# 3x3 convolutions contracted over 128 rows, with partition copies by GpSimd's DMAs

## The chip, the cores and the metric

The kernel runs on one core of a Trainium2 chip. The metric is device time in microseconds (us). The kernel before takes 3841.41 us, the median of three runs (3840.19 to 3842.67). Engines are PE (TensorE, matmuls), DVE (VectorE), ACT (ScalarE), POOL (GpSimd) and SP (SyncE, which issues most DMAs). In the trace PEld is PE's weight loading.

## The reference

The input x has 8 images of 96 channels of 96 x 96 pixels in float32. Two blocks, each with a residual sum, follow one another:

```
x = x + L0(gn(x))       # gn: group norm over 32 groups of 3 channels
x = x + L1(gn(x))

L0: four depthwise 7-tap filters (row, column, two diagonals) -> feats[4]
    context = mean(feats^2); hid = leaky_relu(context @ att1); a = softmax(hid @ att2 over the 4)
    out = conv3x3(sum_d a[d] * feats[d], w_proj)            # 96 -> 96 channels

L1: q, k, v = 1x1 convs; softmax over pixels of q and k; a linear attention; 1x1 conv; 1x1 conv to k, v;
    depthwise 3x3 conv; a second attention whose query goes through an FFT; 1x1 conv
```

In the kernel all linear maps of L1 that follow softmax(q) are folded into one 3x3 convolution per image with 96 x 96 x 9 weights `a32`, applied to E = exp(q). So each image passes through two 3x3 convolutions over 96 channels: the first with the fixed weights `wp` (L0), the second with `a32` (L1).

## The kernel before

Images go through a software pipeline. `steps` calls `start(0)`, `step(0)`, a loop of `step(b)` for b = 1 to 6, `step(7)` and `step(8)`. Every `step(b)` does the second block of image b-1 (`second`) and the first block of image b (`first`) on all five engines; each engine has its own program and keeps its own order, and semaphores order them against each other.

PE's program for one step is: the maxima of k and q (`maxes`), the rows of the FFT, k and v, the context (about 200 us together), the q tiles, then the second convolution of image b-1, then the first convolution of image b, then the group sums. DVE runs beside it: the depthwise taps of image b (L715, in 12 `unit`s of 12 taps of 96x1536), with short pieces for PE between, then `attention_weights` (L750), the last three units of taps with the split of E between them, then `attention` (L806), the products of the four directions with their weights (`products`, L823), and the sums that make x1 (`x1_sum`, L795). During the last of these it starts on image b+1.

A 3x3 convolution (`conv`, L954) goes over 12 blocks `j` of 8 image rows, each in two halves of 4 rows (384 columns). Values are split in a high and a low part in the reduced type that PE reads in one pass: image e_hi + e_lo, weights hi + lo. A half is 27 matmuls over 96 rows: nine taps times (hi x e_hi, hi x e_lo, lo x e_hi). Blocks alternate between two PSUM slots. In the second convolution block j needs the copy of block j-2 out of PSUM, by ACT (`final_copy`, waited for at L1083); in the first convolution it needs the x1 sum of block j-2, by DVE (L1141).

ACT's program between these (L630 to L646) runs in this order: final_copy 0 and 1, `unit_work(b, 9)`, copies 2 and 3, `unit_work(b, 10)`, copies 4 and 5, `unit_work(b, 11)`, copies 6 to HID_AT (7), the softmax of the direction attention, then the high parts of the first convolution's input (`fg_high`), chunk by chunk of 16 rows, with the last copies between. `unit_work(b, u)` squares the unit's two directions and so waits for DVE's taps of unit u.

The direction attention of image b is served by PE inside the second convolution of image b-1: `hidden` (eight tiny matmuls) before half (7, 1), `logits` before half (8, 0). `hidden` waits for DVE's sums over the squares (L811); DVE then waits for `hidden` (L813) and `logits` (L817) before the first product (L832).

DVE's x1 sums stand at fixed places: after chunks 3, 4 and 5 of the products, then between the statistics and the first taps of image b+1. After the twelfth sum the group norm follows, ACT normalizes x1, and the next step begins with `maxes`. POOL issues the loads of `res`, the stores of x1 and the accumulating stores of the result, in program order.

Of the kernel before, what the change touches and what calls it, by code (L numbers as in the profile page):

```python
# [84 lines left out]
HID_AT = 7  # L85
# [4 lines left out]
L0_SMALL, L1_SMALL, GN_SMALL = 8, 21, 7  # L90
# [36 lines left out]
def build(nc, a, out):  # L127
    with ExitStack() as ctx:
# [3 lines left out]
        def sem(name):  # L132
# [8 lines left out]
        e_hi = nc.alloc_sbuf_tensor_at("e_hi", [C, EN], F32R, offset=lo0)  # L141
        e_lo = nc.alloc_sbuf_tensor_at("e_lo", [C, EN], F32R, offset=lo0 + EBYTES)
# [16 lines left out]
        vrow = sb("vrow", [W, VROWS, TR, C])  # L159
        etile = sb("etile", [C, ETILES, TR * W])  # L160
        krow = etile[0:W, 0:VROWS].rearrange("p s (r c) -> p s r c", c=C)
        wp_hi, wp_lo = sb("wp_hi", [C, 9, C], F32R), sb("wp_lo", [C, 9, C], F32R)
        a_hi = sb("a_hi", [C, 9, C], F32R)
# [3 lines left out]
        a_lo = nc.alloc_sbuf_tensor_at("a_lo", [C, 9, C], F32R, offset=k0)  # L167
        bk = nc.alloc_sbuf_tensor_at("bk", [C, 9, C], F32, offset=k0 + ABYTES)

        squares = [nc.alloc_sbuf_tensor_at(f"squares{n}", [C, CR * W], mybir.dt.bfloat16, offset=k0 + n * ABYTES)  # L170
                   for n in range(2)]
        assert CR * W * 2 <= ABYTES
# [70 lines left out]
        fin_ready, fin_copied = sem("fin_ready"), sem("fin_copied")  # L243
        waits_passed = {e.engine: sem(n) for e, n in (
# [13 lines left out]
        def rows(buf, r0, n, dx=0):  # L258

            at = (r0 + 1) * EP + 1 + dx  # L260
            return buf[:, at:at + n * EP].rearrange("p (r c) -> p r c", c=EP)[:, :, 0:W]
# [126 lines left out]
        def _(pool):  # L388
# [5 lines left out]
            def zero_pads():  # L394
                for e in (e_hi, e_lo):
                    f = e[:, :].bitcast(F32)
                    pool.memset(f[:, 0:EP], 0.0).then_inc(pads_zero, 1)
                    pool.memset(f[:, (H + 1) * EP:EN], 0.0).then_inc(pads_zero, 1)
                    pool.memset(f[:, EP:EP + H * EP].rearrange("p (r c) -> p r c", c=EP)[:, :, 0:1], 0.0)\
                        .then_inc(pads_zero, 1)  # L400

# [3 lines left out]
            def step(b, first, second, more):  # L405
                if second:
                    i = b - 1
                    pool.wait_ge(gram_done, i + 1)
                    apart(pool)
                    zero_pads()  # L410
                    pool.wait_ge(l1_small, i * L1_SMALL + 5)
                    pool.tensor_tensor(l1v[:, 1:2], l1v[:, 0:1], consts[:, 1:2], ALU.pow).then_inc(l1_pow, 1)
                    o = image(out, i)
                    for j in range(NG):
                        pool.wait_ge(fin_copied, i * NG + j + 1)
                        if j == 0:
                            apart(pool)
                            pool.wait_ge(x1_stored, (i + 1) * NG * 16)
                        apart(pool)
                        pool.dma_start(o[:, j * GR * W:(j + 1) * GR * W], res[:, j % RES], accum_op=ALU.add)\  # L420
                            .then_inc(out_stored[j % RES], 16)
                if first:
                    if not second:
                        zero_pads()
                    x, o = image(a["x"], b), image(out, b)
                    for j in range(NG + 1):
                        if j < NG:
                            if j < RES:
                                wait(pool, out_stored[j], b * (NG // RES) * 16)
                            else:  # L430
                                wait(pool, x1_done, b * NG + j - RES + 1)
                            apart(pool)
                            pool.dma_start(res[:, j % RES], x[:, j * GR * W:(j + 1) * GR * W])\
                                .then_inc(res_loaded[j % RES], 16)
                        if j >= 1:
                            pool.wait_ge(x1_done, b * NG + j)
                            apart(pool)
                            pool.dma_start(o[:, (j - 1) * GR * W:j * GR * W], x1[0:C, (j - 1) * GR * W:j * GR * W])\
                                .then_inc(x1_stored, 16)
                        if more and j == GN_AT:  # L440
                            start(b + 1)
                    gn_pow(gnx1_small, GN_SMALL, b, 5, 2, gnx1_pow)
# [14 lines left out]
        def _(act):  # L457
# [4 lines left out]
            act.activation(wp_hi[:], wp32[:], ACT.Identity).then_inc(wp_hi_ready, 1)  # L462
# [38 lines left out]
            def square(b, u, d):  # L501
# [7 lines left out]
                act.activation(squares[0 if first_image(b) else 1][:], feat[:, d], ACT.Square, accum_out=sq[:, d, ch:ch + 1]).then_inc(squared, 1)  # L509
# [145 lines left out]
        def _(dve):  # L655
            taps_w = [lambda k: wh[:, k:k + 1], lambda k: wv[:, k:k + 1],
                      lambda k: w45[:, k * KT + k:k * KT + k + 1],
                      lambda k: w135[:, k * KT + KT - 1 - k:k * KT + KT - k]]
            def set_up():
# [3 lines left out]
                dve.wait_ge(wp_hi_ready, 1)  # L663
                dve.tensor_tensor(wp_lo[:], a32[:], wp_hi[:].bitcast(F32), ALU.subtract).then_inc(wp_ready, 1)
# [85 lines left out]
            def attention_weights(i, chain):  # L750
# [41 lines left out]
                dve.wait_ge(a_hi_ready, i + 1)  # L792
                st(dve.tensor_tensor(a_lo[:], a32[:], a_hi[:].bitcast(F32), ALU.subtract))
# [129 lines left out]
        def _(pe):  # L923
# [30 lines left out]
            def conv(i, whi, wlo, done, ready, between={}, low_ready=lambda: None):  # L954

                for j in range(NG):
                    ready(j)
                    for h in range(2):
# [59 lines left out]
            def attention_block(i, between):  # L1018
# [65 lines left out]
                conv(i, a_hi, a_lo, fin_ready, ready, between, lambda: pe.wait_ge(l1_small, i * L1_SMALL + 21))  # L1084
# [23 lines left out]
            def step(b, first, second, more):  # L1108
# [17 lines left out]
                if second:  # L1126
                    attention_block(b - 1, {(HID_AT, 1): hidden, (HID_AT + 1, 0): logits} if first else {})
# [3 lines left out]
                if first:  # L1131
                    if not second:
                        pe.wait_ge(wp_ready, 1)

                    def ready(j):
                        pe.wait_ge(fg_ready, b * NCH + min(NCH - 1, (j + 1) * GR // CR) + 1)
# [5 lines left out]
                    conv(b, wp_hi, wp_lo, conv_ready, ready, {(GN_AT + 1, 0): lambda: start(b + 1)} if more else {})  # L1142
# [58 lines left out]
```

## Time and profile before

| | us |
|---|---|
| median of the runs | 3841.41 |
| the profiled execution | 3844.74 |
| its span, first to last instruction | 3843.1 |
| PE busy | 3649.9 (95%) |
| DVE busy | 3024.8 (79%) |
| ACT busy | 1642.1 (43%) |
| POOL busy | 211.1 (5%) |

Busy time counts every instruction from its start to its end; matmuls are pipelined, so two overlap in the rows and the step from one start to the next is what one costs. "L715" is a line of the kernel. A row of a timeline gives start, duration, engine, line, operation, output<-input, and in brackets how long the engine was idle before it and what ended that.

### The profile page before, as it was taken

What the parts mean: (1) busy time and instruction counts of PE and PEld (TensorE: products, weight loads), DVE (VectorE), ACT (ScalarE), POOL (GpSimd) and SP (SyncE); (2) the same over time, 40 slices, a digit from 0 to 9 for tenths busy, and PEclk for the clock granted to TensorE, in tenths of its full rate; (3) what the DMA queues carried; (4) which work ended last, traced back from release to release, by engine and by line L of the source; (5) the groups of instructions that cost most, each with busy time, mean ns of one, the idle gap of its engine ahead of it and who ended that gap; (6) DMA issues with size and microseconds to landing.
All of it is one profiled execution on the core that took longest, in us unless ns stands there. A gap on an engine that the chain in (4) does not pass through costs nothing.

```text
span 3843.1 us, 59619 instructions
## 1 busy us (share of the span) xinstructions
PE 3649.9 (95%) x22946; PEld 2998.9 (78%) x22946; DVE 3024.8 (79%) x2829; ACT 1642.1 (43%) x2720; POOL 211.1 (5%) x376
## 2 busy tenths in 40 slices
PE   4659999999999999999999999999999999999998
PEld 2348688968789688886889687896888878897977
DVE  7988998789877898779987898878987798854020
ACT  3422682138521584126821386215841268211630
POOL 1001000100001000010001000010000100010000
PEclk8779999999999999999999999999999999999999
DMA  5355222922147231742229222471317422271002
GB/s 116 98 137 132 66 67 35 225 73 69 48 102 182 59 83 42 167 121 67 66 37 226 71 68 51 110 182 48 87 41 173 112 67 66 39 178 32 1 7 31
DMA packets 164730, 344.35 MB, mean 90 GB/s; under 512 B 110336, under 2 KB 110576, under 8 KB 164432
## 3 DMA queue, kind: packets, MB, share of 16 engines
q1 hardware_dynamic: 141392, 255.36, 27.0%
q0 software_dynamic: 23040, 84.95, 10.0%
q8 instruction: 195, 3.19, 0.4%
q14 instruction: 103, 0.84, 0.1%
HBM read 189.27 MB, written 150.99 MB: 89 GB/s over the span
## 4 chain that ended last, share of the span: by engine, by line
PE 56%; DVE 22%; issue 19%; DMA 1%; ACT 1%; SPq 0%; DVEq 0%; POOL 0%; ACTq 0%; POOLq 0%
DVE feat L715 18%; PE banks L970 11%; PE banks L971 11%; PE banks L976 11%; PE banks L985 6%; PE banks L995 3%; PE banks L1053 3%; PE banks L1015 2%; PE banks L1001 2%; PE banks L1002 2%; PE banks L1039 1%; DMA feat<-feats_d 1%; DVE e_lo L747 1%; DVE e_hi L739 1%; PE banks L1008 0%
## 5 line engine op out<-in xcount | busy, mean ns | idle before, releaser
L715 DVE SCALAR_TENSOR_TENSOR feat<-xin,w,feat 96x1536 f32<-96x1536 f32 x540 | 947.1, 1809 | 1.8
L970 PE MATMUL banks<-e_hi,wp_hi 96*96 96x384 f32 x1728 | 587.4, 340 | 24.3 <-DVE e_lo L848 12.2
L970 PE MATMUL banks<-e_hi,a_hi 96*96 96x384 f32 x1728 | 597.7, 347 | 0.0
L971 PE MATMUL banks<-e_lo,a_hi 96*96 96x384 f32 x1728 | 592.9, 344 | 0.0
L971 PE MATMUL banks<-e_lo,wp_hi 96*96 96x384 f32 x1728 | 586.2, 340 | 0.0
L715 DVE SCALAR_TENSOR_TENSOR feat<-xin,wh,feat 96x1536 f32<-96x1536 f32 x288 | 520.7, 1808 | 28.9 <-ACT feat L497 27.2
L715 DVE SCALAR_TENSOR_TENSOR feat<-xin,wv,feat 96x1536 f32<-96x1536 f32 x288 | 520.8, 1808 | 0.0
L509 ACT ACTIVATE squares<-feat 96x1536 bf16<-96x1536 f32 x192 | 285.2, 1485 | 445.0 <-DVE feat L715 443.0
L976 PE MATMUL banks<-e_hi,a_lo 96*96 96x384 f32 (+1 forms) x1728 | 337.5, 339 | 0.0
L976 PE MATMUL banks<-e_hi,wp_lo 96*96 96x384 f32 (+1 forms) x1728 | 335.7, 338 | 0.0
L575 ACT ACTIVATE res<-banks 96x768 f32<-96x768 f32 x96 | 77.2, 804 | 598.7 <-PE banks L976 598.7
L995 PEld LDWEIGHTS banks<-mats,z 96*96 96x96 f32 x3072 | 287.3, 165 | 57.7 <-issue 46.8
L970 PEld LDWEIGHTS banks<-e_hi,wp_hi 96*96 96x96 f32 x1728 | 281.2, 163 | 52.6 <-DVE e_lo L848 13.7
L971 PEld LDWEIGHTS banks<-e_lo,a_hi 96*96 96x96 f32 x1728 | 285.8, 165 | 30.3 <-issue 1.9
L970 PEld LDWEIGHTS banks<-e_hi,a_hi 96*96 96x96 f32 x1728 | 285.4, 165 | 29.9 <-issue 1.9
L971 PEld LDWEIGHTS banks<-e_lo,wp_hi 96*96 96x96 f32 x1728 | 281.5, 163 | 27.6
L976 PEld LDWEIGHTS banks<-e_hi,a_lo 96*96 96x96 f32 x1728 | 279.7, 163 | 26.4
L976 PEld LDWEIGHTS banks<-e_hi,wp_lo 96*96 96x96 f32 x1728 | 278.2, 162 | 26.0
L1039 PE MATMUL banks<-wkv,x 97*96 97x96 f32 x3072 | 295.9, 248 | 0.9
L995 PE MATMUL banks<-mats,z 96*96 96x96 f32 x3072 | 289.8, 248 | 2.6 <-ACT z L538 2.6
L1039 PEld LDWEIGHTS banks<-wkv,x 97*96 97x96 f32 x3072 | 278.6, 165 | 10.5 <-issue 6.1
L724 DVE TENSOR_REDUCE mx<-banks 96x1 f32<-96x512 f32 x288 | 184.7, 681 | 35.4 <-PE banks L985 34.7
(152 smaller groups left out, 4854.1 us busy)
## 6 DMA issues: line engine op xcount, KB each, us to landing
feats_d<-feat SPq DMA_DIRECT2D x160, 576.0 KB, 4.1
feat<-feats_d SPq DMA_DIRECT2D x160, 576.0 KB, 6.8
feat<-in_x SPq DMA_DIRECT2D x48, 576.0 KB, 6.9
res<-in_x POOLq DMA_DIRECT2D x96, 288.0 KB, 4.1
out<-x POOLq DMA_DIRECT2D x96, 288.0 KB, 2.8
out<-res POOLq DMA_DIRECT2D x96, 288.0 KB, 4.3
xin<-in_x SPq DMA_DIRECT2D x32, 792.0 KB, 9.0
xin<-in_x SPq DMA_DIRECT2D x16, 684.0 KB, 10.2
```

Source lines behind the costliest of these rows:

```text
L509: act.activation(squares[0 if first_image(b) else 1][:], feat[:, d], ACT.Square, accum_out=sq[:, d, ch:ch + 1]).then_inc(squared, 1)
L575: act.activation(res[:, j % RES].rearrange("p (h n) -> p h n", h=2), conv_ps[0:C, j % 2, :, 0:TR * W], ACT.Identity).then_inc(fin_copied, 1)
L715: dve.scalar_tensor_tensor(out=dst, in0=src, scalar=taps_w[d](k), in1=dst, op0=ALU.mult, op1=ALU.add).then_inc(tap_done, 1)
L724: dve.tensor_reduce(mx[:, n % 2, n // 2:n // 2 + 1], stage_ps[0:C, n % SLOTS, :], AX.X, ALU.max)\
L970: pe.matmul(dst, whi[:, t, :], rows(e_hi, a0, n, dx), start=(t == CENTRE_FIRST[0]), stop=False)
L971: pe.matmul(dst, whi[:, t, :], rows(e_lo, a0, n, dx), start=False, stop=False)
L976: last = pe.matmul(dst, wlo[:, t, :], rows(e_hi, a0, n, dx), start=False, stop=(t == CENTRE_LAST[-1]))
L985: pe.matmul(ps[0:C, :], w, x1[0:C, t * BANK:(t + 1) * BANK], start=True, stop=True)\
L995: last = pe.matmul(ps[0:H, c * W:(c + 1) * W], z[:, 4 * g + c, :], w_dft, start=(c == 0), stop=(c == 3), skip_group_check=True)
L1001: pe.matmul(d, dcos, s1[:, g % 2, :, 0:NV], start=True, stop=False)
L1039: last = pe.matmul(ps[0:W, r * C:(r + 1) * C], x1[:, h * W:(h + 1) * W], wkv[:, part * C:(part + 1) * C], start=(r == 0), stop=(r == TR - ...
L1053: pe.matmul(gram_ps[0:C, 2 * C:4 * C], t_sp[:, v, 0:C], t_sp[:, v, :], start=(v == 1), stop=(v == NV - 2))
```

## The change

A matmul can contract over 128 rows, and 96 were used. The low-weight products of 32 channels each move into the spare 32 rows: group 1 pairs rows 0 to 95 (hi weights, e_hi) with rows 96 to 127 (lo weights of channels 0 to 31, a copy of e_hi's channels 0 to 31); group 2 pairs (hi weights, e_lo) with (lo weights of channels 32 to 63, a copy of those channels of e_hi). For channels 64 to 95 three copies of e_hi shifted by a row each stand in 96 partitions of a ring of two (`shifted`), so that three matmuls do their nine taps. A half is 9 + 9 + 3 = 21 matmuls.

The copies are made by `fill`: five DMAs for each block, issued from POOL, which wait until block j-2 is done and the high rows are there; PE's block j waits for them. The low weights are made by five DVE operations (`low_part`) in place of one, and the high weights by two ACT copies. `shifted` shares memory with `etile`, the second `squares` buffer moves to `vrow`'s memory. HID_AT goes from 7 to 10, and `hidden` and `logits` now stand before halves (11, 0) and (11, 1).

```
-HID_AT = 7
+HID_AT = 10
-L0_SMALL, L1_SMALL, GN_SMALL = 8, 21, 7
+L0_SMALL, L1_SMALL, GN_SMALL = 8, 25, 7
+SPARE = 32
+SHIFTED = GR * EP + 2
+FILLS = 4
+FILL_DMAS = 5
...
+            def fill(sems, j):
+                lo = 0 if j == 0 else (j * GR + 2) * EP + 1
+                hi = EN if j == NG - 1 else ((j + 1) * GR + 2) * EP + 1
+                done = sems[j % FILLS]
+                pool.dma_start(e_hi[C:C + SPARE, lo:hi], e_hi[0:SPARE, lo:hi]).then_inc(done, 16)
+                pool.dma_start(e_lo[C:C + SPARE, lo:hi], e_hi[SPARE:2 * SPARE, lo:hi]).then_inc(done, 16)
+                for g in range(3):
+                    at = (j * GR + g) * EP
+                    pool.dma_start(shifted[g * SPARE:(g + 1) * SPARE, j % 2, :], e_hi[2 * SPARE:C, at:at + SHIFTED])\
+                        .then_inc(done, 16)
+            def fill_e(i, j):
+                if j < 2:
+                    pool.wait_ge(e_ready, i * U_E + ETILES)
+                else:
+                    pool.wait_ge(fin_ready, i * NG + j - 1)
...
+                pool.wait_ge(e_hi_ready, i * U_E + min(U_E, (j + 1) * GR // TR + 1))
...
+                fill(e_filled, j)
+            def fill_fg(b, j, second):
+                if j >= 2:
+                    pool.wait_ge(conv_ready, b * NG + j - 1)
+                elif second:
+                    pool.wait_ge(fin_ready, (b - 1) * NG + NG - 1 + j)
...
+                pool.wait_ge(fg_hi, b * NCH + min(NCH, (j + 1) * GR // CR + 1))
...
+                fill(fg_filled, j)
...
                     o = image(out, i)
+                    fill_e(i, 0)
+                    fill_e(i, 1)
                     for j in range(NG):
+                        if j + 2 < NG:
+                            fill_e(i, j + 2)
                         pool.wait_ge(fin_copied, i * NG + j + 1)
...
+                    fill_fg(b, 0, second)
+                    fill_fg(b, 1, second)
...
+                        if 1 <= j and j + 1 < NG:
+                            fill_fg(b, j + 1, second)
...
-                act.activation(a_hi[:], a32[:], ACT.Identity).then_inc(a_hi_ready, 1)
+                act.activation(a1[0:C], a32[:], ACT.Identity).then_inc(a_hi_ready, 1)
+                act.activation(a2[0:C], a32[:], ACT.Identity).then_inc(a_hi_ready, 1)
...
+            def low_part(n, w1, w2, w3):
+                if n < 2:
+                    dst, p = (w1, w2)[n], n * SPARE
+                    return dve.tensor_tensor(dst[C:C + SPARE], a32[p:p + SPARE], w1[p:p + SPARE].bitcast(F32), ALU.subtract)
+                g = n - 2
+                return dve.tensor_tensor(w3[g * SPARE:(g + 1) * SPARE], a32[2 * SPARE:C, 3 * g:3 * g + 3, :],
+                                         w1[2 * SPARE:C, 3 * g:3 * g + 3, :].bitcast(F32), ALU.subtract)
...
                         for t in CENTRE_FIRST:
                             dst, a0, n, dx = tap(t)
-                            pe.matmul(dst, whi[:, t, :], rows(e_hi, a0, n, dx), start=(t == CENTRE_FIRST[0]), stop=False)
-                            pe.matmul(dst, whi[:, t, :], rows(e_lo, a0, n, dx), start=False, stop=False)
+                            pe.matmul(dst, w1[:, t, :], rows(e_hi, a0, n, dx, 128), start=(t == CENTRE_FIRST[0]), stop=False)
                         if (j, h) == (0, 0):
-                            low_ready()
+                            second_ready()
                         for t in CENTRE_LAST:
                             dst, a0, n, dx = tap(t)
-                            last = pe.matmul(dst, wlo[:, t, :], rows(e_hi, a0, n, dx), start=False, stop=(t == CENTRE_LAST[-1]))
+                            pe.matmul(dst, w2[:, t, :], rows(e_lo, a0, n, dx, 128), start=False, stop=False)
+                        if (j, h) == (0, 0):
+                            third_ready()
+                        for dx in range(3):
+                            last = pe.matmul(conv_ps[0:C, j % 2, h, 0:TR * W], w3[:, dx, :], shifted_rows(j, h, dx - 1),
+                                             start=False, stop=(dx == 2))
...
-                keep_clock(5, small_ps)
+                keep_clock(4, small_ps)
                 def ready(j):
+                    pe.wait_ge(*filled(e_filled, i, j))
                     pe.wait_ge(e_ready, i * U_E + min(U_E, (j + 1) * GR // TR + 1))
                     if j == 0:
-                        pe.wait_ge(a_hi_ready, i + 1)
+                        pe.wait_ge(l1_small, i * L1_SMALL + 21)
                     elif j >= 2:
                         pe.wait_ge(fin_copied, i * NG + j - 1)
...
-                    attention_block(b - 1, {(HID_AT, 1): hidden, (HID_AT + 1, 0): logits} if first else {})
+                    attention_block(b - 1, {(HID_AT + 1, 0): hidden, (HID_AT + 1, 1): logits} if first else {})
```

## Rows read from the trace of the kernel before

**Rows 1.** The page, part 4: the chain that ended last, by engine.
```profile
PE 56%; DVE 22%; issue 19%; DMA 1%; ACT 1%; SPq 0%; DVEq 0%; POOL 0%; ACTq 0%; POOLq 0%
```

**Rows 2.** Busy time by stretch: length, then PE, PEld, DVE, ACT, POOL, clock, DMA, GB/s.
```profile
1279.40:1726.90 447.50, 440.27 (x2826) 366.96 (x2826) 384.88 (x358) 203.15 (x339) 24.95 (x45) 0.99 0.40 96
...
1606.00:1719.90 113.90, 113.90 (x647) 103.82 (x646) 88.36 (x93) 20.90 (x16) 13.28 (x25) 1.00 0.64 158
```

**Rows 3.** The chain of waits in time, second convolution: start, us, what.
```profile
1559.94 0.32 PE banks L971
...
1563.46 0.32 PE banks L970
...
1580.08 1.60 PE banks L976 x9
...
1584.90 1.59 PE banks L976 x9
```

**Rows 4.** Timeline of PE: `hidden` (L1115) and `logits` (L1122).
```profile
1558.58 0.80 PE L1115 MATMUL banks<-l0v,att 96*48 96x1 f32 x8 [3.03 <-DVE l0v L811]
...
1566.30 0.84 PE L1122 MATMUL banks<-hid,att 48*96 48x1 f32 x8
```

**Rows 5.** Timeline of ACT: final_copy 6.
```profile
1558.03 0.79 ACT L575 ACTIVATE res<-banks 96x768 f32<-96x768 f32 x1
```

**Rows 6.** Timeline of DVE: low weights, first product, last x1 sum.
```profile
1482.11 1.05 DVE L793 TENSOR_TENSOR a_lo<-a,a_hi 96x864 fp32r<-96x864 f32 x1 [1.06 <-ACT a_hi L584]
...
1568.57 1.02 DVE L832 TENSOR_SCALAR feat<-feat,l0v 96x1536 f32<-96x1536 f32 x1
...
1719.87 0.95 DVE L800 TENSOR_TENSOR x<-banks,res 96x768 f32<-96x768 f32 x1 [3.74 <-PE banks L976]
```

**Rows 7.** DVE's waits, 1568.5 to 1721: total us, times, longest.
```profile
DVE x L800 <- PE banks L976: 8.8, 5, 3.7
DVE feat L832 <- DMA feat<-feats_d: 7.3, 5, 2.6
...
DVE gstat L684 <- PE banks L952: 3.2, 1, 3.2
```

**Rows 8.** Timeline of DVE, first image: set_up, first product, third sum, group sums, last sum.
```profile
25.40 1.03 DVE L664 TENSOR_TENSOR wp_lo<-a,wp_hi 96x864 fp32r<-96x864 f32 x1
...
234.22 1.01 DVE L832 TENSOR_SCALAR feat<-feat,l0v 96x1536 f32<-96x1536 f32 x1
...
298.79 0.95 DVE L800 TENSOR_TENSOR x<-banks,res 96x768 f32<-96x768 f32 x1
...
319.50 0.15 DVE L684 COPY gstat<-banks 96x2 f32<-96x2 f32 x1 [3.17 <-PE banks L952]
...
376.70 0.95 DVE L800 TENSOR_TENSOR x<-banks,res 96x768 f32<-96x768 f32 x1 [3.74 <-PE banks L976]
```

**Rows 9.** DVE's waits in the first image, 234.2 to 378.
```profile
DVE x L800 <- PE banks L976: 5.4, 4, 3.7
```

**Rows 10.** Timeline of DVE, last first convolution: first product, last sum.
```profile
3358.25 1.02 DVE L832 TENSOR_SCALAR feat<-feat,l0v 96x1536 f32<-96x1536 f32 x1
...
3509.37 0.95 DVE L800 TENSOR_TENSOR x<-banks,res 96x768 f32<-96x768 f32 x1 [7.19 <-PE banks L976]
```

**Rows 11.** Timeline of POOL: issues of DMAs.
```profile
29.99 1.24 POOL L433 DMA_DIRECT2D res<-in_x  x2
...
1588.13 1.17 POOL L420 DMA_DIRECT2D out<-res  x1 [8.90 <-ACT res L575]
...
1721.53 0.51 POOL L438 DMA_DIRECT2D out<-x  x1 [8.69 <-DVE x L800]
```

**Rows 12.** Timeline of DVE at the slow issue of rows 11.
```profile
1588.17 1.02 DVE L832 TENSOR_SCALAR feat<-feat,l0v 96x1536 f32<-96x1536 f32 x1 [1.65 <-DMA feat<-feats_d]
```

**Rows 13.** The page, part 6: POOL's stores, KB each, us from issue to landing.
```profile
out<-x POOLq DMA_DIRECT2D x96, 288.0 KB, 2.8
out<-res POOLq DMA_DIRECT2D x96, 288.0 KB, 4.3
```

More of the change, by code:

```diff
@@ L158, in build @@
         res = sb("res", [C, RES, GR * W])
[L159 to L160 removed]
+        VBYTES = VROWS * TR * C * 4
+        arena5 = sb("arena5", [128, VBYTES // 4])
+        v0 = nc.sbuf_base - VBYTES
+        vrow = nc.alloc_sbuf_tensor_at("vrow", [W, VROWS, TR, C], F32, offset=v0)
+        TBYTES = max(ETILES * TR * W, 2 * SHIFTED) * 4
+        arena4 = sb("arena4", [128, -(-TBYTES // 32) * 8])
+        t0 = nc.sbuf_base - -(-TBYTES // 32) * 32
+        etile = nc.alloc_sbuf_tensor_at("etile", [C, ETILES, TR * W], F32, offset=t0)
+        shifted = nc.alloc_sbuf_tensor_at("shifted", [3 * SPARE, 2, SHIFTED], F32R, offset=t0)
         krow = etile[0:W, 0:VROWS].rearrange("p s (r c) -> p s r c", c=C)
[L162 to L163 removed]
+        wp1, wp2 = sb("wp1", [128, 9, C], F32R), sb("wp2", [128, 9, C], F32R)
+        wp3 = sb("wp3", [3 * SPARE, 3, C], F32R)
         ABYTES = 9 * C * 4
@@ L166, in build @@
         k0 = nc.sbuf_base - 2 * ABYTES
-        a_lo = nc.alloc_sbuf_tensor_at("a_lo", [C, 9, C], F32R, offset=k0)
+        a1 = nc.alloc_sbuf_tensor_at("a1", [128, 9, C], F32R, offset=k0)
+        a2 = nc.alloc_sbuf_tensor_at("a2", [128, 9, C], F32R, offset=k0 + ABYTES)
+        a3 = sb("a3", [3 * SPARE, 3, C], F32R)
         bk = nc.alloc_sbuf_tensor_at("bk", [C, 9, C], F32, offset=k0 + ABYTES)
-        squares = [nc.alloc_sbuf_tensor_at(f"squares{n}", [C, CR * W], mybir.dt.bfloat16, offset=k0 + n * ABYTES)
-                   for n in range(2)]
-        assert CR * W * 2 <= ABYTES
+        squares = [nc.alloc_sbuf_tensor_at(f"squares{n}", [C, CR * W], mybir.dt.bfloat16, offset=at)
+                   for n, at in enumerate((k0, v0))]
+        assert CR * W * 2 <= min(ABYTES, VBYTES)
         wkv = sb("wkv", [C + 1, 2 * C])
@@ L243, in build @@
         fin_ready, fin_copied = sem("fin_ready"), sem("fin_copied")
+        fg_filled = [sem(f"fg_filled{n}") for n in range(FILLS)]
+        e_filled = [sem(f"e_filled{n}") for n in range(FILLS)]
         waits_passed = {e.engine: sem(n) for e, n in (
@@ L508, in square @@
                 wait(act, squared, b * DIRS * NCH + q * DIRS + d)
-                act.activation(squares[0 if first_image(b) else 1][:], feat[:, d], ACT.Square, accum_out=sq[:, d, ch:ch + 1]).then_inc(squared, 1)
+                act.activation(squares[0 if first_image(b) or u <= LEAD else 1][:], feat[:, d], ACT.Square, accum_out=sq[:, d, ch:ch + 1]).then_inc(squared, 1)
             def unit_work(b, u, part=None):
@@ L662, in set_up @@
                 dve.wait_ge(consts_set, 5)
-                dve.wait_ge(wp_hi_ready, 1)
-                dve.tensor_tensor(wp_lo[:], a32[:], wp_hi[:].bitcast(F32), ALU.subtract).then_inc(wp_ready, 1)
+                dve.wait_ge(wp_hi_ready, 2)
+                for n in range(LO_PARTS):
+                    low_part(n, wp1, wp2, wp3).then_inc(wp_ready, 1)
             def x_stats(b, n0, n1):
@@ L791, in attention_weights @@
                                      a_ps[0:C, :, 0:9 * C // 2], l1v[:, 11:12], None, ALU.mult))
-                dve.wait_ge(a_hi_ready, i + 1)
-                st(dve.tensor_tensor(a_lo[:], a32[:], a_hi[:].bitcast(F32), ALU.subtract))
+                dve.wait_ge(a_hi_ready, 2 * i + 1)
+                st(low_part(0, a1, a2, a3))
+                for n in range(1, LO_PARTS):
+                    if n == 1:
+                        dve.wait_ge(a_hi_ready, 2 * i + 2)
+                        apart(dve)
+                    st(low_part(n, a1, a2, a3))
             def x1_sum(b, j):
@@ L952, in group_sums, with conv @@
                 pe.matmul(small_ps[0:C, 500:502], group, mv[:], start=True, stop=True).then_inc(done, 1)
-            def conv(i, whi, wlo, done, ready, between={}, low_ready=lambda: None):
+            def conv(w1, w2, w3, done, ready, between={}, second_ready=lambda: None, third_ready=lambda: None):
                 for j in range(NG):
@@ L1141, in ready @@
                             pe.wait_ge(x1_done, b * NG + j - 1)
-                    conv(b, wp_hi, wp_lo, conv_ready, ready, {(GN_AT + 1, 0): lambda: start(b + 1)} if more else {})
+                    conv(wp1, wp2, wp3, conv_ready, ready, {(GN_AT + 1, 0): lambda: start(b + 1)} if more else {})
                     keep_clock(3, stage_ps[:, SLOTS - 1])
```

29 lines of the change are left out of this document (21 added, 8 removed).

## The prediction

> **What bounds the kernel now.** First the chain of waits by engine [rows 1]: PE holds 56% of it, DVE 22%. That is an average over stages, so next the busy time of one image (1279 to 1727 us, 447.5 us, of which there are six alike between the first image and the last) and of its first convolution [rows 2]: PE is busy 440 of 447 us, DVE 385, and while the first convolution runs (1606 to 1720) PE is busy 113.9 of 113.9, DVE 88. A cut of matmuls therefore pays until the next engine in line is late. To see which, I read the timelines of PE, ACT and DVE through both convolutions in order, and DVE's waits.
>
> The second convolution of image i-1 runs from about 1483 beside DVE's last taps of image i. Then come the four small steps of the direction attention: DVE sums the squares, PE multiplies `hidden` (L1115), half a block later `logits` (L1122), and 2.27 us after `logits` starts, DVE begins the products (1566.30 to 1568.57) [rows 4, 6]. PE had waited only 3.0 us for DVE there. From the first product to the last x1 sum is one DVE sequence, 151.3 us (1568.57 to 1719.87) [rows 6], in which DVE waits 8.8 + 3.2 us for PE [rows 7]. After the last sum the group norm releases the next image. So PE sets the pace now, but DVE follows with only 12 us to spare in this stretch.
>
> **The matmuls.** Half a block is 27 matmuls in 4.82 us (1580.08 to 1584.90), 0.1785 us each [rows 3]. With 21 it is 3.75, a block 7.5 instead of 9.6. I price a 128-row matmul as a 96-row one: it streams the same columns. Sixteen convolutions of 24 halves lose 2304 matmuls, 411 us of PE time; the question is how much of it is on the path.
>
> **The copies.** Each block needs five more DMAs on POOL, 960 in all, issued when the block two before it is done, so they have the 7.5 us of the block between. POOL starts 0.7 us after the event it waits for (sum ended 1720.82, store 1721.53), two issues back to back take 1.24, and a transfer without accumulation lands 2.8 us after issue [rows 6, 11, 13]. 0.7 + 4 x 0.62 + 2.8 = 6.0 us, inside 7.5. No row shows a copy within SBUF. Below, 0.7 + 4 x 0.51 + 2.8 = 5.5; above, with every issue as slow as the slowest here (1.17) and the 4.3 us landing of accumulating stores, 9.7. I take 6.0, since plain stores are nearest, and hide it behind the block between. At 9.7 a block costs (9.7 + 7.5) / 2 = 8.6. POOL's other queue entries move little: behind a waiting fill stand the stores of `res` and `x1`, which ACT needs only three blocks later and after the last block, and the `res` loads, which still come 15 us or more ahead of the first sum. The moves of buffers (the ring over `etile`, `squares` over `vrow`) issue nothing; the one wait they add, fills 0 and 1 of the second convolution behind the split of `etile`, ends in DVE's program before the weights are made, and PE cannot start before these. No cost.
>
> The 1.17 us issue stands beside a DVE tensor_scalar of 1.02 us that began 0.04 us after it; both end within 0.1 us [rows 11, 12]. The Trainium skill (SBUF — State Buffer, "Who interferes with whom") says that copy, cast and tensor_scalar on VectorE can take the port pair that it shares with GpSimd for the whole instruction, which starves the writing of GpSimd's DMA descriptors; it speaks against POOL as the issuer, and the row agrees. By the rule a fill's five issues lengthen when they meet the casts of the split; by the row's 0.4 us each that is 8.0 instead of 6.0, and some 5 us more in all, through rival 1.
>
> **The weights.** The low parts are five DVE operations in place of one of 1.05 us [rows 6]: two of that size and three with a third of the elements (0.36 each, scaled), with the chain's gaps 3.3, so 2.3 us more before DVE's taps go on. PE's own start does not move: the clock-keeping matmuls ended later than the first low part will. Bounds 1 and 4 us. For the first image set_up sits on DVE's path: +2.3 us from L664 [rows 8].
>
> **Where `hidden` moves.** This is the largest term. PE's block j needs final_copy j-2 (L1083), and ACT's order is fixed (L635 to L640): copies 0, 1, the squares of unit 9, copies 2, 3, unit 10, copies 4, 5, unit 11, then the rest. Copy 6 therefore waits for DVE's last tap, however fast PE is: it ran at 1558.03 to 1558.82 [rows 5]. Before, PE was at block 7 by then and nobody noticed. Now PE finishes block 7 near 1555 and stands until 1558.8 + 2.3 = 1561.1. Before, `hidden` was served in block 7; the edit puts it at the start of block 11, behind blocks 8, 9 and 10. The restart is slow: after the 3.0 us stall fourteen matmuls took 0.32 us each (1559.94 and 1563.46 are the first and the last of twelve; the ones before and after are slow in part) [rows 3], so + 14 x 0.14 = 2.0. `hidden` starts at 1561.1 + 2.0 + 3 x 7.5 = 1585.6, `logits` 0.8 + 3.75 later at 1590.1, the first product at 1592.4: 23.8 us later than 1568.57. Without slow restart and longer set of low parts it is +19.5; with fills of 9.7 us about +27.
>
> **What the path gives back.** From the products on, DVE no longer waits for PE: conv1 blocks take 7.5 us and DVE's sums come 5.5 to 13 us apart. The sequence of the first image, which has no second convolution beside it, shows the length: 142.5 us (234.22 to 376.70) [rows 8] with 5.4 + 3.2 us of waits for PE [rows 8, 9], 134.5 without them, keeping 0.6 as latency. The same from the steady image: 151.3 - 12.0 + 0.6 = 139.9. I take 136, nearer to the first image, since there too the second convolution is over when the products begin, and a little above it for the fills' traffic. The end of the image moves by 23.8 - (151.3 - 136) = +8.5 (7.0 to 12.4). PE then has idled some 6 us before the next maxes, and its slow restart adds 1.5 (0 to 2). So +10 us per image, six times: +60.
>
> The last image with a first convolution has no next image's taps between its sums (3358.25 to 3509.37) [rows 10]; there PE paces and DVE waits. Products start 23.8 later, the third sum comes 64.6 after (298.79 - 234.22) [rows 8], then 1.0, eight blocks of 7.5 and a slow restart of 2.0: 3509.6, no change. The first image: +2.3 - 8.6 + 0.6 + 1.5 = -4.2. The closing second convolution has nothing beside it and takes the whole gain: 24 x 6 x 0.1785 = -25.7.
>
> Sum: -4.2 + 60 + 0 - 25.7 = +30 on the profiled execution's 3844.7 (span 3843.1 and 1.6 around it), 3875; the runs' median lies 3.3 below it, so **3871 us**.
>
> **Rivals.** (1) The fills are late. For it: five issues in a row, lengthened beside DVE; against it: 1.5 us of slack. At 9.7 us: `hidden` 3.3 later six times, +9 in the last image (8 x 1.1), +13 in the close: +42, 3914. (2) The second convolution runs free, and `hidden` comes at 1483 + 11 x 7.5 = 1565.7 with products at 1572.5. Shift +4, image -15.3 + 4 + 1.5 = -10, six times -60; last image -20, first -4, close -26: 3735. For it: PE waited only 3 us there. Against it: copy 6 stands behind the squares in ACT's program, and the row shows it starting as these end. It decides if block 8 can start before 1559. (3) The products' loads, now without the other convolution's stores beside them, no longer hold up the first product of each chunk: 7.3 us of DVE's waits [rows 7] go, 128.7 remain of 136, the image moves by +2.7 and not by 10, and the sum is -4.2 + 16 - 25.7 = -14, 3827. Against it: the first image has no such stores either and its stretch is only 3 to 5 us shorter. (4) PE bounds everywhere and all 411 us go: 3430; DVE's 385 us per image alone forbids most of that.
>
> **Numbers.** Forecast 0.58 (own range 3845 to 3895), late fills 0.20, free convolution 0.12, loads 0.08, all matmuls 0.02. A measurement of this kernel tells about 0.2% (8 us) from no change. Slower: 0.20 and nearly all of the forecast, 0.72; same 0.05; faster 0.23 (rivals 2 to 4 and a little of the forecast). The range leaves out rivals 2 and 4 and the far end of 1: 3795 to 3935.
>
> **What would show it.** `hidden` at PE's last block some 25 us after DVE's L811, with DVE idle between; PE idle before block 8, which begins as copy 6 ends; products to last sum 134 to 140 us with almost no wait for PE; blocks of the closing convolution 7.5 us apart (8 or more: late fills). I am wrong if block 8 starts before the last squares, if the products begin less than 10 us later in the image, or if PE's blocks wait on fills.

## The result and the profile after

The changed kernel takes 4015.74 us (4010.62 to 4016.73), the kernel before 3841.79: a ratio of 1.0451, 95% interval 1.0432 to 1.0469. Forecast were 3871 us and a range up to 3935: the direction was right, the size was not; 174 us came where 30 were expected.

The page of the changed kernel: busy time (part 1), the chain by engine (part 4), the matmuls of the first convolution that begin its half blocks (part 5: busy time and mean ns | idle time of the engine before them, and what ended most of it), and three rows of DMA issues (part 6: KB each, median us from issue to landing).
```profile
PE 3376.7 (84%) x20626; PEld 2713.7 (68%) x20626; DVE 3043.7 (76%) x2865; ACT 1648.5 (41%) x2729; POOL 694.1 (17%) x1336
...
PE 32%; DVE 30%; issue 24%; DMA 10%; ACT 2%; POOL 1%; SPq 0%; DVEq 0%; ACTq 0%; POOLq 0%
...
L1052 PE MATMUL banks<-e_hi,wp 128*96 128x384 f32 x1728 | 399.2, 383 | 366.4 <-DMA shifted<-e_hi 248.0
...
feat<-feats_d SPq DMA_DIRECT2D x160, 576.0 KB, 8.3
shifted<-e_hi POOLq DMA_DIRECT2D x576, 97.2 KB, 2.7
feat<-in_x SPq DMA_DIRECT2D x48, 576.0 KB, 9.9
```
PE lost 273 us of work and its hold on the chain (56% before [rows 1]); DMA went from 1% to 10%. In the first convolution PE stood 248 us over the run for the copies, which the prediction had named as a sign of being wrong; in the second it stood for none (106.8 us idle before its half blocks, 105.8 of them for ScalarE's copies out of PSUM).

Busy time by stretch, as in [rows 2]: one whole image, and in it the stretch from the first product to the last x1 sum; the third row is this stretch in the kernel before.
```profile
1347.40:1825.00 477.60, 409.29 (x2538) 333.72 (x2537) 386.87 (x362) 203.61 (x340) 85.04 (x165) 0.92 0.51 115
1661.00:1817.80 156.80, 108.84 (x526) 95.11 (x524) 116.78 (x110) 26.00 (x19) 43.34 (x85) 0.81 0.87 199
...
1568.57:1719.87 151.30, 151.30 (x860) 138.06 (x859) 117.00 (x110) 28.25 (x22) 16.19 (x29) 1.00 0.71 175
```
The image is 30 us longer while DVE has only 2 us more to do. In the second row DVE works 117 us of 157, PE's granted clock is 0.81 of 2.4 GHz on the mean, so it ran at 1.2 for part of it (1.00 before), and the DMA engines are busy for 0.87 of the time (0.71 before).

The timeline of DVE through this image: the last step before `hidden`, `hidden` itself, the first product, the third sum, the statistics, the group sums, the last sum.
```profile
1629.41 0.17 DVE L893 TENSOR_SCALAR l0v<-l0v 96x4 f32<-96x4 f32 x1
...
1654.95 0.15 DVE L895 COPY hid<-banks 48x1 f32<-48x1 f32 x1 [25.37 <-PE banks L1203]
...
1661.02 1.02 DVE L914 TENSOR_SCALAR feat<-feat,l0v 96x1536 f32<-96x1536 f32 x1
...
1738.85 0.94 DVE L882 TENSOR_TENSOR x<-banks,res 96x768 f32<-96x768 f32 x1
...
1758.93 0.21 DVE L758 SCALAR_TENSOR_TENSOR mv<-mv 96x1 f32<-96x1 f32 x1
...
1766.34 0.15 DVE L761 COPY gstat<-banks 96x2 f32<-96x2 f32 x1 [7.18 <-PE banks L1034]
...
1817.80 0.94 DVE L882 TENSOR_TENSOR x<-banks,res 96x768 f32<-96x768 f32 x1
```
DVE stands 25 us for `hidden`, as forecast, and the reason is the forecast one: PE's block 8 of the second convolution waits for ScalarE's copy 6, which runs right behind the last squares.
```profile
1627.60 1.48 ACT L575 ACTIVATE squares<-feat 96x1536 bf16<-96x1536 f32 x1 [0.15 <-DVE feat L792]
...
1629.08 1.49 ACT L641 ACTIVATE res<-banks 96x768 f32<-96x768 f32 x2
```
```profile
1629.92 3.19 PE L1052 MATMUL banks<-e_hi,a 128*96 128x384 f32 x9 [6.77 <-ACT res L641]
```
But from the first product to the last sum it then takes 156.8 us, where [rows 6] had 151.3 and 136 were forecast. DVE's waits between them (total, times, longest); the last two rows are from the kernel before and go with [rows 7]:
```profile
DVE feat L914 <- DMA feat<-feats_d: 10.2, 4, 3.6
DVE feat L924 <- DMA feat<-feats_d: 8.0, 6, 2.2
DVE gstat L761 <- PE banks L1034: 7.2, 1, 7.2
DVE acc L924 <- DMA feat<-feats_d: 4.6, 3, 2.0
...
DVE feat L842 <- DMA feat<-feats_d: 2.3, 2, 1.3
...
DVE acc L842 <- DMA feat<-feats_d: 1.6, 2, 1.1
```
No x1 sum of this image waits for PE any more (8.8 us before), which the forecast had counted on. In its place the products wait 22.8 us for their loads (11.2 before) and the group norm 7.2 us for its sums (3.2 before).

Why the sums are late is seen on PE and GpSimd. PE's timeline, blocks 4 and 5 of the first convolution; after it GpSimd's issues of the same time:
```profile
1741.11 3.19 PE L1052 MATMUL banks<-e_hi,wp 128*96 128x384 f32 x9 [3.13 <-DMA shifted<-e_hi]
1744.10 2.99 PE L1057 MATMUL banks<-e_lo,wp 128*96 128x384 f32 x9
...
1747.46 1.76 PE L1052 MATMUL banks<-e_hi,wp 128*96 128x384 f32 x9
...
1756.77 3.19 PE L1052 MATMUL banks<-e_hi,wp 128*96 128x384 f32 x9 [5.42 <-DMA shifted<-e_hi]
...
1766.09 1.83 PE L1052 MATMUL banks<-e_hi,wp 128*96 128x384 f32 x9
```
```profile
1742.38 0.53 POOL L503 DMA_DIRECT2D out<-x  x1 [9.09 <-issue]
1743.12 0.52 POOL L496 DMA_DIRECT2D res<-in_x  x1 [0.21 <-issue]
1743.88 0.50 POOL L432 DMA_DIRECT2D e_hi<-e_hi  x1 [0.24 <-issue]
...
1744.87 1.46 POOL L436 DMA_DIRECT2D shifted<-e_hi  x3
```
The five copies for block 5 go out at 1743.88 to 1746.33, behind a store of x1 (L503) that waits for the third sum (ended 1739.79; the store begins 2.6 us after that, for which the profile shows no reason). PE can start on them only at 1756.77, 10.4 us after the last issue, and stands until then. Then it restarts slowly: nine matmuls in 3.19 us instead of 1.76. So block 6, ahead of which the group sums stand, begins at 1766, 7 us after DVE had the statistics (1758.93 + 0.21).

### The profile page after: what moved, and what is told of

The parts are those of the page before. It is cut to its first block, busy times and chain, and to the rows that moved or that the text cites. A ratio compares the mean times of both kernels' runs of the same rounds, so it can differ in the third digit from the quotient of the medians.

```text
span 4014.5 us, 56603 instructions
## 1 busy us (share of the span) xinstructions
PE 3376.7 (84%) x20626; PEld 2713.7 (68%) x20626; DVE 3043.7 (76%) x2865; ACT 1648.5 (41%) x2729; POOL 694.1 (17%) x1336
## 4 chain that ended last, share of the span: by engine, by line
PE 32%; DVE 30%; issue 24%; DMA 10%; ACT 2%; POOL 1%; SPq 0%; DVEq 0%; ACTq 0%; POOLq 0%
DVE feat L792 22%; DMA feat<-feats_d 8%; PE banks L1071 6%; PE banks L1052 5%; PE banks L1057 4%; PE banks L1081 3%; PE banks L1139 3%; PE banks L1101 2%; PE banks L1087 2%; DMA shifted<-e_hi 2%; PE banks L1088 2%; DVE acc L924 2%; PE banks L1061 1%; DVE x L882 1%; DVE feat L924 1%
## 5 line engine op out<-in xcount | busy, mean ns | idle before, releaser
L1052 PE MATMUL banks<-e_hi,wp 128*96 128x384 f32 x1728 | 399.2, 383 | 366.4 <-DMA shifted<-e_hi 248.0
L1052 PEld LDWEIGHTS banks<-e_hi,wp 128*96 128x96 f32 x1728 | 315.3, 187 | 417.9 <-issue 251.1
L792 DVE SCALAR_TENSOR_TENSOR feat<-xin,wh,feat 96x1536 f32<-96x1536 f32 x288 | 520.2, 1806 | 28.9 <-ACT feat L563 27.3
L1052 PE MATMUL banks<-e_hi,a 128*96 128x384 f32 x1728 | 363.0, 357 | 106.8 <-ACT res L641 105.8
L1052 PEld LDWEIGHTS banks<-e_hi,a 128*96 128x96 f32 x1728 | 291.3, 171 | 149.9 <-ACT res L641 97.1
L1057 PE MATMUL banks<-e_lo,wp 128*96 128x384 f32 (+1 forms) x1728 | 370.6, 363 | 0.0
L1057 PE MATMUL banks<-e_lo,a 128*96 128x384 f32 (+1 forms) x1728 | 347.3, 346 | 0.0
L1057 PEld LDWEIGHTS banks<-e_lo,wp 128*96 128x96 f32 x1728 | 311.6, 181 | 33.3
L1057 PEld LDWEIGHTS banks<-e_lo,a 128*96 128x96 f32 x1728 | 290.2, 169 | 28.8
L436 POOL DMA_DIRECT2D shifted<-e_hi x576 | 287.0, 519 | 9.6 <-issue 9.4
L1125 PEld LDWEIGHTS banks<-wkv,x 97*96 97x96 f32 x3072 | 278.6, 165 | 10.4 <-issue 6.1
L432 POOL DMA_DIRECT2D e_hi<-e_hi x192 | 101.4, 528 | 818.9 <-PE banks L1061 405.8
```

Source lines behind the costliest of these rows:

```text
L432: pool.dma_start(e_hi[C:C + SPARE, lo:hi], e_hi[0:SPARE, lo:hi]).then_inc(done, 16)
L436: pool.dma_start(shifted[g * SPARE:(g + 1) * SPARE, j % 2, :], e_hi[2 * SPARE:C, at:at + SHIFTED])\
L792: dve.scalar_tensor_tensor(out=dst, in0=src, scalar=taps_w[d](k), in1=dst, op0=ALU.mult, op1=ALU.add).then_inc(tap_done, 1)
L1052: pe.matmul(dst, w1[:, t, :], rows(e_hi, a0, n, dx, 128), start=(t == CENTRE_FIRST[0]), stop=False)
L1057: pe.matmul(dst, w2[:, t, :], rows(e_lo, a0, n, dx, 128), start=False, stop=False)
L1125: last = pe.matmul(ps[0:W, r * C:(r + 1) * C], x1[:, h * W:(h + 1) * W], wkv[:, part * C:(part + 1) * C], start=(r == 0), stop=(r == TR - ...
```

## The experiments

The comparison is one table, each number from the timelines: us from the image's first maxes to its first product and from there to the start of its last x1 sum, means over the six like images; the first maxes of all (the end of the first image); and the runs' median. All ratios are to the kernel before.

| kernel | to products | products to last sum | first image | median | ratio, 95% interval |
|---|---|---|---|---|---|
| before | 289.1 | 151.3 | 383.0 | 3841 | |
| changed | 314.2 | 154.4 | 398.6 | 4015.7 | 1.0451 (1.0432, 1.0469) |
| changed, `hidden` at block 8 | 291.7 | 158.7 | 396.5 | 3890.7 | 1.0134 (1.0117, 1.0151) |
| before, `hidden` at block 11 | 317.3 | 144.9 | 382.5 | 3993.0 | 1.0394 (1.0376, 1.0411) |
| second convolution only, block 11 | 313.0 | 144.9 | 382.4 | 3944.6 | 1.0271 (1.0254, 1.0288) |
| second only, block 8 | 291.2 | 150.6 | 384.2 | 3829.9 | 0.9968 (0.9956, 0.9981) |
| changed, small copies, block 11 | 314.3 | 143.2 | 382.0 | 3924.8 | 1.0216 (1.0200, 1.0232) |
| changed, small copies, block 8 | 291.0 | 149.5 | 383.5 | 3816.9 | 0.9938 (0.9923, 0.9953) |
| second only, block 8, unread copies | 291.2 | 158.5 | 393.7 | 3899.6 | 1.0157 (1.0142, 1.0173) |
| second only, early `hidden` | 290.9 | 151.6 | 383.3 | 3835.2 | 0.9985 (0.9976, 0.9994) |
| changed, copies ahead of stores | 314.2 | 151.2 | 392.9 | 3992.6 | 1.0402 (1.0377, 1.0426) |
| small copies ahead of stores | 314.0 | 139.1 | 383.4 | 3903.1 | 1.0165 (1.0148, 1.0182) |
| second only, block 10, three copies | 290.5 | 145.7 | 383.7 | 3791.3 | 0.9871 (0.9855, 0.9888) |
| the same, group sums earlier | 291.3 | 148.5 | 385.5 | 3815.1 | 0.9931 (0.9915, 0.9948) |

**Is the move of `hidden` what it was priced at?** In the changed kernel it went back to block 8; in the kernel before it alone was moved.
```
# changed kernel                         # kernel before
-HID_AT = 10                             -HID_AT = 7
+HID_AT = 7                              +HID_AT = 10
                                         -{(HID_AT, 1): hidden, (HID_AT + 1, 0): logits}
                                         +{(HID_AT + 1, 0): hidden, (HID_AT + 1, 1): logits}
```


> The changed kernel, but hidden and logits stand at PE's blocks 8 (first and second half) instead of 11. Theory A (the move holds DVE idle 24 us per image, and what follows it is a sequence of DVE's own): products begin about 22 us earlier, the second convolution's last blocks then run beside them and give back up to 8 us: 14 to 22 us per image for seven images, 3862 to 3918 us. Theory B (the DMA engines are full after the products begin, and the loads come when they come): less than 5 us per image, 3980 to 4016.

> The kernel before, with 27 matmuls and no copies; only hidden and logits stand at block 11 (both halves). Theory A: hidden 3.5 blocks of 9.6 us later, 33 us, of which the shorter sequence after it gives back 11: some 22 us per image, 3970 to 4010 us. Theory B (the slowdown comes from the copies' traffic, and the idle time before the products is made up behind them): under 8 us per image, below 3900.

125 us came back in the first and 152 us were lost in the second: theory A in both. The table shows the two halves of it: products 22.5 us earlier against 4.3 longer after them; 28.2 us later against 6.4 shorter.

**Does the rest of the sum hold without the first convolution's copies?** In these two only the second convolution changed; the first has 27 matmuls again.
```
-conv(wp1, wp2, wp3, conv_ready, ...)
+conv(wp1, wp2, None, conv_ready, ...)     # 9 x (high, low) and 9 low weights, 96 rows
-fill_fg(b, j + 1, second)                 # and fill_fg(b, 0), fill_fg(b, 1)
```


> Only the second convolution takes 21 matmuls and copies; the first has the 27 of before and no copies; hidden and logits at block 11. If the missing term is the first convolution's copies, the products' sequence falls from 156.8 to 136 to 142 us and the sum of the prediction holds without its first-image term: 3865 to 3900 us. If the copies of the first convolution cost nothing, the time stays within 15 us of the changed kernel: 4000 to 4030.

> As the one before, but hidden and logits at blocks 8 (both halves). Theory A: products begin 4 us later than before the change, PE reaches the first convolution 15 us earlier, and the sequence behind gains 0 to 12 us; last image some 15 us shorter, closing convolution 24 us: 3740 to 3830 us, faster than the kernel before. If the second convolution's copies disturb the taps or the products' loads by more than this: over 3842.

The first fell between the two answers. Its sequence is 144.9, not 136 to 142, since DVE still waits 5.4 + 3.1 us in it for the longer matmul blocks; against the changed kernel 71 us are gone, so the first convolution's part costs that much net. Without the waits for PE the sequence is 144.9 - 8.5 = 136.4: the forecast's 136 holds where the first convolution makes no copies. The second is 11 us faster than the kernel before: a small gain, at the slow edge of the expectation. All of it comes from the closing convolution (304.9 us instead of 327.5); the six images are 1.6 us longer each, the first and the last with a first convolution 1.2 and 1.7.

**Bytes, or issues and latency?** The first convolution's copies shrink, with all else in place; the spare rows are zeroed once in the first image, and the sums of the first convolution are no longer the reference's, since most copied rows are stale.
```
-pool.dma_start(e_hi[C:C+SPARE, lo:hi], ...)
+pool.dma_start(e_hi[C:C+SPARE, lo:lo + 16], ...)    # so in all five, first convolution only
```


> The changed kernel, but each of the first convolution's five copies per block moves 16 elements of a partition instead of 770; issues, semaphores, waits and matmuls are all there (most of the copied rows are stale, so the first convolution's sums are not the reference's). If the bytes are the missing term, the sequence from the products to the last sum falls from 154 to the predicted 136 to 141 us in every image: 14 to 18 us times eight, 3870 to 3905 us. If the issues, the waits or the copies' fixed latency are: under 4 us per image, 3985 to 4016.

> The same with hidden and logits at block 8 (both halves). Bytes theory: as much below the 3891 us of the changed kernel with hidden at block 8, 110 to 140 us, so 3750 to 3780 us. Otherwise over 3860.

With `hidden` at block 11 the gain was 91 us, short of the 110 expected but far past the other answer; the sequence fell by 11.3 us and the first image by 16.6. With `hidden` at block 8 it was 74, where 110 to 140 were expected: 3816.9 lies between the two answers. The stretch between first product and last sum in the first of the two (busy time, clock, DMA share, GB/s as above), and DVE's waits in it:
```profile
1627.00:1772.60 145.60, 103.02 (x526) 89.95 (x524) 116.79 (x110) 26.03 (x19) 42.95 (x85) 0.87 0.72 174
```
```profile
DVE feat L922 <- DMA feat<-feats_d: 8.2, 5, 3.0
DVE gstat L769 <- PE banks L1042: 7.5, 1, 7.5
DVE feat L932 <- DMA feat<-feats_d: 3.9, 5, 1.5
```
The products' waits are near those of before, the DMA share too (0.72; 0.87 with full copies, 0.71 before). The wait for the group sums is not gone at all: bytes don't make it.

**The traffic by itself.** The first convolution is the old one, and nobody reads its copies.
```
 conv(wp1, wp2, None, conv_ready, ...)
+fill_fg(b, 0), fill_fg(b, 1), fill_fg(b, j + 1)     # as in the change; POOL waits for copies j - 2 itself
```


> The first convolution with the 27 matmuls of before and hidden at block 8, as in the run of 3830 us, but GpSimd still makes the first convolution's full copies, which no matmul waits for or reads. If the harm is that the copies slow the loads that the products and the statistics wait for, the sequence grows by 6 to 10 us of its 150 and the time is 3870 to 3910 us. If it is PE's waiting for late copies, nothing waits here: 3825 to 3845 us.

Copies that no matmul waits for cost 70 us (3829.9 to 3899.6), 7.9 of them in each image's sequence. The same two views:
```profile
1599.90:1758.20 158.30, 144.82 (x791) 130.21 (x790) 117.05 (x110) 28.34 (x22) 50.81 (x98) 0.96 0.88 209
```
```profile
DVE feat L919 <- DMA feat<-feats_d: 13.9, 5, 4.3
DVE feat L797 <- ACT feat L569: 8.5, 1, 8.5
DVE x L887 <- DMA res<-in_x: 6.6, 2, 4.7
```
The loads of the products and of `res` come late, and with the next image's input late its first taps are too (8.5 us, 3.1 without the copies). SyncE's loads, which GpSimd's program doesn't order, land later (part 6 of the page without the copies, then with them):
```profile
feat<-feats_d SPq DMA_DIRECT2D x160, 576.0 KB, 7.8
...
feat<-in_x SPq DMA_DIRECT2D x48, 576.0 KB, 6.9
```
```profile
feat<-feats_d SPq DMA_DIRECT2D x160, 576.0 KB, 8.5
...
feat<-in_x SPq DMA_DIRECT2D x48, 576.0 KB, 9.7
```
That the traffic alone slows loads, with no matmul waiting for a copy, is shown. The `res` loads stand in GpSimd's program behind its waits for copies j - 2, so how much of their lateness is traffic and how much is order was not separated.

**An early `hidden`.** As the kernel with the second convolution only and block 8, but `hidden` in the second half of block 7.
```
-{(HID_AT + 1, 0): hidden, (HID_AT + 1, 1): logits}
+{(HID_AT, 1): hidden, (HID_AT + 1, 0): logits}
```


> Only the second convolution changed, hidden back in the second half of block 7 and logits in block 8, as before the change. PE then takes hidden before it stands for the copy of block 6: products begin some 2 us earlier in seven images, 3810 to 3825 us. If the restart after the stall only moves behind hidden, no gain: 3826 to 3835.

No gain: 3835.2, and 290.9 instead of 291.2 to the products. The stand only moved: PE now waits some 10 us before `hidden` for DVE's sums over the squares, where it had waited 6.8 to 7.1 us at block 8 for copy 6 (six like images).

**Why the group sums are late.** GpSimd's turn j of the first convolution loads `res`, makes the copies for block j+1, then waits for a sum to store a block. The store goes one turn later; the second of these kernels also has the small copies.
```
-for j in range(NG + 1): ...; if j >= 1: pool.wait_ge(x1_done, b * NG + j); store block j - 1
+for j in range(NG + 2): ...; if j >= 2: pool.wait_ge(x1_done, b * NG + j - 1); store block j - 2
```


> The changed kernel; in GpSimd's program of the first convolution the store of each finished block is written one turn later, so that the copies for block j+1 stand behind the sum of block j-3 instead of j-2. If GpSimd's order holds the copies back (they waited for a sum that PE's block does not need), PE begins blocks 4 to 6 some 5 us earlier and DVE's wait for the group sums falls from 7.2 to 0.5 to 3 us: 4 to 7 us per image for seven images, 3966 to 3988 us. If the copies only queue behind the other traffic of their queue and land no earlier: 4005 to 4020.

> The same order with 16 elements per partition in the first convolution's copies (most of the copied rows are stale, as in the other kernel with small copies). If the missing term is bytes plus late group sums and nothing else, the sequence from the products to the last sum is the predicted 135 to 138 us and the time 3868 to 3885 us. If the group sums stay late, 3915 to 3926.

DVE's waits for group sums over the whole run, in the changed kernel and then with the copies ahead of the stores:
```profile
DVE gstat L761 <- PE banks L1034: 54.1, 16, 7.6
```
```profile
DVE gstat L761 <- PE banks L1034: 12.8, 16, 4.0
```
41 us of waits went, so the order made them. 23 us of time came back (28 to 50 were expected): with the full copies some of it is given back to loads (over the run, waits of `acc` from 27.0 to 41.6 us and of the next image's first taps from 27.3 to 50.6). With small copies the sequence is 139.1, close to the forecast's 136, and the wait for group sums is 1.4 to 3.2 us in the six like images (5.9 to 7.5 with the old order). The 3903 us lie above the range expected: the order was to give 6 us in each of seven or eight images, and gave 4.1 in the sequences of six and nothing in the first and the last.

**A version that gains.** Only the second convolution; ScalarE copies three blocks between the squares of the last units, so that PE need not stand at block 8 for copy 6; `hidden` at block 10. The two changes were made together, and no run has one without the other.
```
-HID_AT = 10                     +HID_AT = 9
-copies(j, j + 2); j += 2        +copies(j, j + 3); j += 3
# the second kernel also:  -{(GN_AT + 1, 0): lambda: start(b + 1)}  +{(GN_AT, 1): lambda: start(b + 1)}
```


> Only the second convolution changed; ScalarE copies three blocks, not two, between the squares of the last units, so that block 8 need not wait for the last squares, and hidden and logits stand at block 10. If copy 6 behind the squares is all that stops the second convolution, PE is at block 10 when the squares are summed, products begin at 289 us of the image as before the change, and with one block and a half left beside them the sequence falls from 150 to about 145 us: 3780 to 3800 us. If ScalarE then holds the last taps up, or PE waits for DVE's split of the exponentials, products begin later and the time is over 3825.

> As the one before, with the next image's group sums half a block earlier (second half of block 5). DVE waits 3.1 us for them in every image; half a block is 4.8 us, PE may stand up to 2 us for the statistics. If DVE sets the pace there: 1 to 2.5 us per image less, 8 to 18 us below the one before. If PE does: no change, within 5 us.

The first is the fastest here, 3791.3 us, 1.3% below the kernel before. Its timeline of ACT shows the last squares directly followed by a copy (of block 9, no longer 6), and DVE's shows `hidden` without a stall:
```profile
1550.58 1.48 ACT L570 ACTIVATE squares<-feat 96x1536 bf16<-96x1536 f32 x1 [0.15 <-DVE feat L786]
...
1552.06 0.79 ACT L636 ACTIVATE res<-banks 96x768 f32<-96x768 f32 x1
```
```profile
1553.17 0.15 DVE L889 COPY hid<-banks 48x1 f32<-48x1 f32 x1 [0.61 <-PE banks L1204]
...
1560.77 1.02 DVE L908 TENSOR_SCALAR feat<-feat,l0v 96x1536 f32<-96x1536 f32 x1
```
The second lost 24 us against the first, which neither expected answer had. DVE's waits over the whole run, in the first and in the second:
```profile
DVE x L876 <- PE banks L1056: 98.4, 38, 7.6
...
DVE gstat L755 <- PE banks L1028: 26.4, 16, 3.1
```
```profile
DVE x L876 <- PE banks L1056: 159.5, 57, 7.6
...
DVE gstat L755 <- PE banks L1028: 8.1, 16, 0.7
```
The wait for the sums went (18 us) and 61 us of waits for matmul blocks came: PE, which had not stood for the statistics, now stands 1.9 us for them in each of seven images, and with 27 matmuls the next x1 sums wait for it.

## Why the prediction was right and wrong

**Which step failed.** By the maxes that end each image, the 171.4 us between the two profiled spans are: first image +15.6 (forecast -4.2), six images +28.6 each (forecast +10), last image with a first convolution +8.6 (forecast 0), closing convolution -24.4 (forecast -25.7). The step that failed is "What the path gives back": its term "products to last x1 sum 136 us" measured 154.4, and 18.4 us six times are 110 of the 141 us missing. The first and the last image miss in the same stretch: 154.2 where the sum had 134.5, and 136.2 where it had 127.6, with PE's blocks at 7.5 us and no stand. Behind the term stands the step under "The copies", which let a copy land 2.8 us after its issue, inside the 7.5 us of the block between; in the first convolution it does not, and PE stood 248 us for copies.

**What stands in its place.** The runs take it apart:
- 11.3 us: the bytes of the copies (154.4 to 143.2 with small ones; 7.9 by unread traffic alone). The first image lost 16.6 the same way, the last 9.4 (its period 456.7 against 447.4 with small copies, where no change was forecast and 448.2 stood before). I had put the traffic at 1.5 us (136 for 134.5), though the stretch already moved 158 GB/s at a DMA share of 0.64 [rows 2] and its loads already kept DVE waiting [rows 7].
- 4.1 us: copies issued late (143.2 to 139.1). I wrote that they go out "when the block two before it is done", and looked at what stands behind them in GpSimd's queue, not at what stands ahead: a store that waits for DVE's sum. With PE faster than DVE that sum is the later of the two. The copies' landing, too, was 6.9 us (median of the `shifted` copies) in this stretch and not 2.8, and PE restarts slowly at its blocks 0 to 5, not at none: at the two before the group sums the first halves took 6.35 and 5.46 us (1741.11 to 1747.46, 1756.77 to 1762.23) instead of 3.74. I had counted the 3.2 us for group sums [rows 7] as gone; they became 7.2.
- 3.1 us are left between 139.1 and 136; on average 2.3 are still a wait for the group sums, the rest was not taken apart.

**What was right.** Half a block of 21 takes 3.74 us (3914.77 to 3918.51 in the close; 3.75 forecast), so a matmul over 128 rows costs what one over 96 does. `hidden` stands 306.2 us after the maxes by the forecast, 306.9 to 308.8 in the trace; products came 25.1 us later on average (23.8), and the cause, copy 6 behind the squares, is in the trace and was shown by the kernel that takes it away. In the six like images the x1 sums wait at most 2.2 us for PE; in the last they wait 39.6 us (62.6 before), and there the forecast had PE set the pace. The low parts delayed the taps by 2.7 us (6.02 us from the weights to the next tap, 3.35 before; 2.3 forecast, inside its bounds). The closing convolution gained what was said, and no copy is late in it.

**The rivals.** (1) Copies are late, but in the first convolution, by a busy queue and GpSimd's order, and not in the second by long issues: by this rival the closing stage would have lost 13 us, and it lost none. (2) The free second convolution needs another order on ScalarE; made so, and with the first convolution left alone, it gives 3791. (3) The loads' waits went from 11.2 to 22.8 us, not to nothing. (4) Both convolutions with nearly free copies and `hidden` at block 8 come to 3816.9; PE's saved 273 us are mostly beside DVE.

**Issues or traffic.** L436's issues took 489 to 1212 ns, with a median of 510, and with the issues kept and the bytes gone 91 us came back, so long issues were not the cause. They do exist: of the 960 copy issues eight took 0.90 to 1.27 us, one in each image, each beside a tensor_scalar of DVE of 1.02 to 1.10 us (L914), and none of the others, those beside casts among them, took over 0.75. The Trainium skill (SBUF — State Buffer, "Who interferes with whom") says that VectorE's tensor_scalar and casts can hold up GpSimd's writing of descriptors; the eight issues agree, the casts here do not show it. What did bear on the time was the traffic: with full copies on GpSimd's queue the products' loads on SyncE's landed in 8.4 us, with small ones in 7.1 (median of 20 in the stretch). The Trainium skill (DMA: Bandwidth & Descriptors, "Issuing engines are not separate DMA queues") says that DMAs interleave on the same 16 DMA engines whichever engine issued them; the runs agree.

## What to carry to other kernels

A copy on chip is traffic like any other: before adding one, look at the DMA share of the stretch in which it runs, and at which loads already make an engine wait there. For every instruction added to an engine's in-order program look at what stands ahead of it as well as behind. When PE's work shrinks, gains come where PE alone sets the pace: here at once in the close, and in the second convolution only after ScalarE's order was changed too. Leave the stages that DVE or the loads pace as they are.

## What was not expected of the hardware

In the stretch with the first convolution, `shifted` copies of 2 KB landed 5.3 us after issue (median), those of 97 KB 6.9: most of a copy's landing time there is not its bytes. Copies that no matmul read or waited for cost 70 us over the run. After a wait of 5.4 us PE's next nine matmuls took 3.19 us instead of 1.76, and over the stretch, at a granted clock of 0.81, the mean matmul took 0.207 us (108.84 / 526), where PE without pauses, at 1.00, took 0.176 (151.30 / 860): part of what the shorter count saves goes into the slower clock.
